# The complement masks of the second attention layer move to GpSimd, and its values are split by their upper halves

## What is computed

```python
seq = (x @ W_seq).reshape(N, H, DH)                      # N 2048, H 16, DH 32
score1 = jnp.einsum('nhd,d->hn', seq, a1)
score2 = jnp.einsum('nhd,d->hn', seq, a2)
scores = score1[:, :, None] + score2[:, None, :]
scores = jax.nn.leaky_relu(scores, negative_slope=0.2)
scores = scores + (1.0 - adj)[None, :, :] * MASK_VAL     # MASK_VAL -65500
attn = jax.nn.softmax(scores, axis=-1)
hidden = jnp.einsum('hij,jhd->ihd', attn, seq).reshape(N, D_IN)
hidden = hidden @ W_out + b_out
return jax.nn.elu(hidden)
```

## Time and profile before

| | us |
|---|---|
| median of 3 runs | 1329.88 |
| lowest, highest | 1329.02, 1330.25 |
| the profiled execution | 1327.29 |
| its span in the trace | 1325.7 |
| PE busy | 1152.6 (87%) |
| DVE busy | 974.9 (74%) |
| ACT busy | 797.1 (60%) |
| POOL busy | 169.9 (13%) |

### The profile page before, as it was taken

One profiled execution on the slowest core, in us unless ns is written; L12 is line 12 of the kernel. 1 busy time (PEld: TensorE's weight loads), 2 busy tenths in 40 slices (PEclk: granted clock), 3 DMA queues, 4 the chain that ended last, 5 costly groups with the idle time before them and its releaser, 6 DMA issues. The chain is left out here.

```text
span 1325.7 us, 24575 instructions
## 1 busy us (share of the span) xinstructions
PE 1152.6 (87%) x10450; PEld 784.7 (59%) x10450; DVE 974.9 (74%) x1340; ACT 797.1 (60%) x779; POOL 169.9 (13%) x182
## 2 busy tenths in 40 slices
PE   4797668889888888888699399999999999999797
PEld 3343323333333333334355299999999999999543
DVE  2310137999999999988189679999889988999265
ACT  1321526556665556553144588888888888888032
POOL 2777700000000000000066100000000000000011
PEclk9899789998898898899899699999999999999799
DMA  9530151221112110000476210000110000000321
GB/s 358 73 25 1 20 113 18 42 42 37 39 34 42 34 35 34 17 16 24 128 177 109 74 34 34 34 34 34 44 55 34 34 34 34 34 34 3 112 111 71
DMA packets 31625, 75.00 MB, mean 57 GB/s; under 512 B 5413, under 2 KB 10402, under 8 KB 29474
## 3 DMA queue, kind: packets, MB, share of 16 engines
q1 hardware_dynamic: 21426, 49.53, 10.7%
q0 software_dynamic: 10096, 23.97, 10.5%
HBM read 78.76 MB, written 15.61 MB: 71 GB/s over the span
## 5 line engine op out<-in xcount | busy, mean ns | idle before, releaser
L959 ACT ACTIVATE s_masks<-s_s1b,s 128x2048 fp8e4<-128x2048 f32 x208 | 396.7, 1987 | 0.0
L1104 PE MATMUL psum<-s_V,s_masks 128*128 128x198 bf16 x2560 | 352.3, 249 | 15.2 <-DVE s_masks L1001 15.2
L1105 PE MATMUL psum<-s_V,nadjT 128*128 128x99 bf16 x2560 | 347.0, 209 | 0.0
L1104 PEld LDWEIGHTS psum<-s_V,s_masks 128*128 128x128 fp8e4 x2560 | 249.9, 98 | 15.7 <-issue 15.4
L1105 PEld LDWEIGHTS psum<-s_V,nadjT 128*128 128x128 fp8e4 x2560 | 250.2, 98 | 0.0
L461 PE MATMUL psum<-h,s_WT 128*128 128x512 f32 x512 | 246.1, 606 | 0.6
L502 ACT ACTIVATE s_exp<-s_exp,s_negm 128x1536 f32<-128x1536 f32 x96 | 150.7, 1570 | 101.3 <-DVE s_negm L597 101.3
L441 PE MATMUL psum<-f_qk 64*128 64x512 f32 x576 | 159.5, 693 | 54.9 <-DVE s_negm L597 54.9
L1001 DVE TENSOR_TENSOR s_masks<-s_masks,adjT 128x512 uint32<-128x512 uint32 x256 | 169.4, 681 | 49.5 <-ACT s_masks L959 47.0
L597 DVE CUSTOM_DVE_ANT_0 s_exp<-psum,f_low 128x1536 f32<-128x1536 f32 x96 | 164.7, 1752 | 16.7 <-PE psum L441 16.2
L588 DVE SCALAR_TENSOR_TENSOR s_W<-s_exp,s_r,s_W 128x1536 f32<-128x1536 f32 x96 | 174.4, 1817 | 2.2
(11 more groups left out here) (127 smaller groups left out, 1140.5 us busy)
## 6 DMA issues: line engine op xcount, KB each, us to landing
s_s1b<-s_rows SPq DMA_DIRECT2D x16, 1024.0 KB, 4.6
s_adj<-in_adj POOLq DMA_DIRECT2D x16, 512.0 KB, 5.2
rel_planes<-s_zero POOLq DMA_DIRECT2D x3, 2304.0 KB, 23.0
f_rel<-rel_planes SPq DMA_DIRECT2D x36, 192.0 KB, 3.5
s_x<-x SPq DMA_DIRECT2D x6, 1024.0 KB, 11.0
h<-in_x SPq DMA_DIRECT2D x4, 1024.0 KB, 21.1
f_adj<-in_adj POOLq DMA_DIRECT2D x16, 256.0 KB, 5.5
s_x<-in_x SPq DMA_DIRECT2D x16, 256.0 KB, 2.6
```

Of the source, the lines that this page charges most:

```text
L959: act.activation(masks[:, j, :], s1b[b][:, :], ACT.Relu, bias=t["s2"][:, n, 0, j:j + 1], scale=BIG, saturate=False).then_inc(signs, 1)
L1104: pe.matmul(out, masks[:, j, cols], V[:, b, j, :, :], **first)
L1105: last = pe.matmul(out[:, :, DZ:CZ], nadjT[:, j, cols], V[:, b, j, :, DZ:CZ], **then)
```

## The change

In stage 3, `negated_adj` and `nadjT` go. In stage 4:
- POOL makes the far mask of every source tile as a 32-bit add of `adjT` and the mask (`far`), after `mask_ready` of that tile. A byte 0x40 + 0x40 is 0x80, which is minus zero; 0x40 + 0 is 2.0. No carry crosses a byte. The far masks are positive now, so `join` adds.
- PE does two short products for every source tile and waits for `far_ready` at each.
- `VECTOR_SIGN` is (2, 6, 10, 14): four compares on DVE, twelve on ACT.
- The split is by the upper 16 bits of each f32 (`upper`, a bf16 view with a step of two of the now doubled `tmp`): ACT copies upper halves into `V` (`pack`), DVE takes the upper half off without waiting for that copy. PE waits for `split` and `packed`.
- The places of sums, scale, join, invert, norm and take-offs among the masks move.

```diff
-VECTOR_SIGN = (3, 8, 13)
-FAR = (1, 4, 6, 9, 11, 14)
+VECTOR_SIGN = (2, 6, 10, 14)
@@ stage3, vector queue
-            def negated_adj(it):
-
-                dve.wait_ge(adj_out_a, it.at(1))
-                dve.wait_ge(adj_out_v, it.at(1))
-                dve.tensor_scalar(nadjT[:, :, it.rows()].bitcast(U32), adjT[:, :, it.rows()].bitcast(U32),
-                                  SIGNS, None, ALU.bitwise_xor).then_inc(t["lasting"], 1)
@@ stage4
-    tmp = sb("tmp", [P, NT, CZ])
+    tmp = sb("tmp", [P, 2, NT, CZ])
+    upper = tmp[:, :, :, :].bitcast(BF16).rearrange("p s j (c w) -> p s j c w", w=2)[:, :, :, :, 1]
-    fars = sb("fars", [P, len(FAR), N], F8)
+    fars = sb("fars", [P, NT, N], F8)
@@ gpsimd queue
+            def far(n, j):
+
+                pool.wait_ge(mask_ready, NT * n + j + 1)
+                pool.tensor_tensor(fars[:, j, :].bitcast(U32), adjT[:, j, :].bitcast(U32),
+                                   masks[:, j, :].bitcast(U32), ALU.add).then_inc(far_ready, 1)
+            for n in range(HB):
+                for j in range(NT):
+                    far(n, j)
@@ scalar queue
-                act.activation(V[:, b, :, p, :], tmp[:, :, :], ACT.Copy).then_inc(hi_out if p == 0 else mid_out, 1)
+                act.activation(V[:, b, :, p, :], upper[:, p, :, :], ACT.Copy).then_inc(packed, 1)
-                    if j in (5, 11) and n < HB - 1:
-                        part(n + 1, 1 - b, 0 if j == 5 else 1)
+                    if j in (9, 14) and n < HB - 1:
+                        pack(n + 1, 1 - b, 0 if j == 9 else 1)
@@ vector queue
-                    dve.wait_ge(split, m)
+                    dve.wait_ge(packed, 2 * m - 1)
+                    dve.wait_ge(rest, m)
@@ take_off
-                dve.wait_ge(hi_out if p == 0 else mid_out, m + 1)
-                out = tmp[:, :, :] if p == 0 else V[:, b, :, 2, :]
-                dve.tensor_tensor(out, tmp[:, :, :], V[:, b, :, p, :], ALU.subtract).then_inc(rest if p == 0 else split, 1)
+                dve.wait_ge(*((value, 2 * (m + 1)) if p == 0 else (rest, m + 1)))
+                if p == 0 and m > 0:
+                    dve.wait_ge(packed, 2 * m)
+                    dve.wait_ge(split, m)
+                if p == 1 and m >= 2:
+                    dve.wait_ge(psum_done[1], m - 1)
+                out = tmp[:, 1, :, :] if p == 0 else V[:, b, :, 2, :]
+                dve.tensor_tensor(out, tmp[:, p, :, :], upper[:, p, :, :], ALU.subtract).then_inc(rest if p == 0 else split, 1)
-            def far(n, j):
-
-                dve.wait_ge(mask_ready, NT * n + j + 1)
-                dve.tensor_tensor(fars[:, FAR.index(j), :].bitcast(U32), nadjT[:, j, :].bitcast(U32),
-                                  masks[:, j, :].bitcast(U32), ALU.bitwise_xor).then_inc(far_ready, 1)
@@ join
-                dve.tensor_tensor(hid[:, :, :], sums[:, :, 0, :], sums[:, :, 1, :], ALU.subtract).then_inc(joined, 1)
+                dve.tensor_tensor(hid[:, :, :], sums[:, :, 0, :], sums[:, :, 1, :], ALU.add).then_inc(joined, 1)
@@ head: j of sum_parts 0, scale, join, invert, norm: 2, 7, 8, 9, 11 -> 3, 13, 14, 15, 15; take-offs 6, 12 -> 9, 11
@@ tensor queue
-                if j in FAR:
-                    pe.wait_ge(far_ready, len(FAR) * n + FAR.index(j) + 1)
+                pe.wait_ge(far_ready, NT * n + j + 1)
-                    if j in FAR:
-                        pe.matmul(out[:, :, 0:DZ], masks[:, j, cols], V[:, b, j, :, 0:DZ], **first)
-                        last = pe.matmul(out[:, :, DZ:CZ], fars[:, FAR.index(j), cols], V[:, b, j, :, DZ:CZ], **then)
-                    else:
-                        pe.matmul(out, masks[:, j, cols], V[:, b, j, :, :], **first)
-                        last = pe.matmul(out[:, :, DZ:CZ], nadjT[:, j, cols], V[:, b, j, :, DZ:CZ], **then)
+                    pe.matmul(out[:, :, 0:DZ], masks[:, j, cols], V[:, b, j, :, 0:DZ], **first)
+                    last = pe.matmul(out[:, :, DZ:CZ], fars[:, j, cols], V[:, b, j, :, DZ:CZ], **then)
@@ head
                 pe.wait_ge(split, n + 1)
+                pe.wait_ge(packed, 2 * (n + 1))
```

More of the change, by code:

```diff
@@ L57 @@
 NEAR = 2.0
-SIGNS = 0x80808080
 ADJ_RING = 6
@@ L643, in stage3 @@
     sem = lambda name: c.enter_context(nc.semaphore(name))
-    seq, adjT, nadjT = t["seq"], t["adjT"], t["nadjT"]
+    seq, adjT = t["seq"], t["adjT"]
     xs = sb("s3_x", [P, NT, D])
@@ L779, in _ @@
                 score(At(0, n - 2))
-                negated_adj(At(0, n - 2))
             score(At(0, NT - 2))
-            negated_adj(At(0, NT - 2))
             turned_adj(At(0, NT - 1))
             score(At(0, NT - 1))
-            negated_adj(At(0, NT - 1))
             steps_done = [0]
@@ L925, in stage4 @@
         sem("signs"), sem("vector_signs"), sem("mask"), sem("far"), sem("mask_used"))
-    value, hi_out, rest, mid_out, split = sem("value"), sem("hi"), sem("rest"), sem("mid"), sem("split")
+    value, rest, split, packed = sem("value"), sem("rest"), sem("split"), sem("packed")
     psum_done, bank_free = ([sem(f"{n}{i}") for i in range(2)] for n in ("psum_done", "bank_free"))
@@ L939, in _, with pack @@
                 load(n + 2, n % 2)
+        @block.gpsimd
+        def _(pool):
+            def far(n, j):
[5 more added lines that the diff above has]
+                    far(n, j)
         @block.scalar
         def _(act):
-            def part(m, b, p):
+            def pack(m, b, p):
                 act.wait_ge(*((value, 2 * (m + 1)) if p == 0 else (rest, m + 1)))
@@ L960, in head @@
                                        saturate=False).then_inc(signs, 1)
-                    if j in (5, 11) and n < HB - 1:
-                        part(n + 1, 1 - b, 0 if j == 5 else 1)
-            part(0, 0, 0)
-            part(0, 0, 1)
+                    if j in (9, 14) and n < HB - 1:
+                        pack(n + 1, 1 - b, 0 if j == 9 else 1)
+            pack(0, 0, 0)
+            pack(0, 0, 1)
             for n in range(HB):
@@ L975, in values @@
                 if m > 0:
-                    dve.wait_ge(split, m)
-                dve.tensor_tensor(tmp[:, :, :].rearrange("p j (k z) -> p j k z", k=2)[:, :, :, 0:DH],
-                                  seq[:, :, None, m * DH:(m + 1) * DH].to_broadcast([P, NT, 2, DH]),
+                    dve.wait_ge(packed, 2 * m - 1)
+                    dve.wait_ge(rest, m)
+                out = tmp[:, 0, :, :].rearrange("p j (k z) -> p j k z", k=2)
+                dve.tensor_tensor(out[:, :, :, 0:DH], seq[:, :, None, m * DH:(m + 1) * DH].to_broadcast([P, NT, 2, DH]),
                                   t["e"][:, :, :, m:m + 1].rearrange("p k j o -> p j k o").to_broadcast([P, NT, 2, DH]),
                                   ALU.mult).then_inc(value, 1)
-                dve.tensor_copy(tmp[:, :, :].rearrange("p j (k z) -> p j k z", k=2)[:, :, :, DH:DZ],
-                                t["e"][:, :, :, m:m + 1].rearrange("p k j o -> p j k o")).then_inc(value, 1)
+                dve.tensor_copy(out[:, :, :, DH:DZ], t["e"][:, :, :, m:m + 1].rearrange("p k j o -> p j k o")).then_inc(value, 1)
             def take_off(m, b, p):
-                dve.wait_ge(hi_out if p == 0 else mid_out, m + 1)
-                out = tmp[:, :, :] if p == 0 else V[:, b, :, 2, :]
-                dve.tensor_tensor(out, tmp[:, :, :], V[:, b, :, p, :], ALU.subtract).then_inc(rest if p == 0 else split, 1)
+                dve.wait_ge(*((value, 2 * (m + 1)) if p == 0 else (rest, m + 1)))
[6 more added lines that the diff above has]
+                dve.tensor_tensor(out, tmp[:, p, :, :], upper[:, p, :, :], ALU.subtract).then_inc(rest if p == 0 else split, 1)
             def vector_sign(n, b, j):
@@ L1047, in head @@
                     mask(n, j)
-                    if j - 1 in FAR:
-                        far(n, j - 1)
                     if n > 0:
-                        if j == 2:
+                        if j == 3:
                             sum_parts(n - 1, 0)
@@ L1054, in head @@
                             sum_parts(n - 1, 1)
-                        if j == 7:
+                        if j == 13:
                             scale(n - 1)
-                        if j == 8:
+                        if j == 14:
                             join(n - 1)
-                        if j == 9:
+                        if j == 15:
                             invert(n - 1)
-                        if j == 11:
                             norm(n - 1)
@@ L1065, in head @@
                             values(n + 1)
-                        if j == 6:
+                        if j == 9:
                             take_off(n + 1, 1 - b, 0)
-                        if j == 12:
+                        if j == 11:
                             take_off(n + 1, 1 - b, 1)
@@ L1287, in build @@
                     sb = lambda name, shape, dt=F32: attention.enter_context(nc.sbuf_tensor(name, shape, dt))
```

(2 more changed lines are left out.)

## The result

The changed kernel takes 1457.59 us (median of 4 runs, 1456.5 to 1458.78); the kernel before, run beside it, 1330.07. The ratio is 1.0958 (95% interval 1.0939 to 1.0977): 127.5 us slower. Forecast were 1469 us and 139 us slower.

What follows compares the result with a forecast made beforehand. PE bounds stage 4 at 30.0 us a head; DVE and POOL excluding each other would make it 39.4. The last reduction then comes 139.6 us later, less 0.3 in stage 3: 1466.6, 1469 as median; range 1370 to 1620.

Steps and rivals of the forecast that it cites:

- PE's sum: Stage 4: all 32 steps of a head become short, 24.0 us, 5.8 us less; alone worth 93 us.
- The inference on the port: Stage 4: whatever fetches two SBUF words a cycle, two-input DVE instructions too, can't run beside a POOL product or add.
- The word rates drawn from rows 7 and 8: DVE's two-input instructions, L765 and compares fetch two words in about 1.05 to 1.1 ns; reductions fetch one.
- T: Full stage 4 head: 20.2 us of DVE port work, 20.0 of POOL, handovers -1.9, reductions +1.1; 39.4 us.
- the port's work: DVE work of a stage 4 head that excludes POOL's: 24.1 less reductions, reciprocal and small copy, 20.2 us.
- The integer add: POOL's add in stage 4 costs what stage 3's product does: 1.25 us each, 20.0 us a head.
- Rivals 2 and 4: Stage 4 add dearer, from 1.6 us, 1559 us total (chance 0.08); or as cheap as DVE's, 0.60, no change (0.03).
- ACT's copies with a step: Stage 4 copies reading every second bf16 keep their price, 0.97 us, within 0.5 either way.
- Start of stage 4: Take-off 0 no longer waits for ACT's copy; first mask at about 752.4, some 1.1 us sooner.
- Stage 3: Dropping sixteen L765 from DVE gains nothing, as PE bounds the loop; only the last one saves 0.3 us.
- Rival 3: PE in stage 4 cools to its lower clock throughout, 48.0 us a head, 1607 us in total; chance 0.05.
- PE's waits: In stage 4 PE waits in every source tile for its far masks, as a sign of the forecast.

## Why the prediction was right

*What bounds, PE's sum.* Right. The short steps alone, shown without the adds, gave 85 us where the sum had 93 for PE alone and ACT's 24.9 us a head as the next bound; the head came to 24.5.

*The inference on the port.* Right, and now shown rather than argued: a two-input instruction is held by a reading POOL instruction (masks of 1318 ns), it is not by a writing one (691 ns), and reductions aren't by either. The word rates drawn from rows 7 and 8 pointed the right way. They were incomplete on one point: I spoke of "two SBUF words a cycle" fetched and of nothing else, while the compares and the copy are held by a POOL that reads nothing. For those, POOL's writing is enough.

*The size.* T was put at 39.4 us and is 38.7. The terms: DVE without POOL 24.1 against 24.5 (without adds; ACT is busy throughout there, so that run alone is no test to 0.4 us). Most of this is the reductions: I took 1.8 us for each, and from start to start one takes 1.95 (917.13 to 919.08). POOL's add was 1.25 less 0.12 of handover, 1.13, and is 1.07. 20.2 + 16 x 1.07 + 1.1 = 38.4 us; the 0.3 that are missing are twice the 0.15 of the reductions. So T holds two errors of opposite sign, 16 x 0.06 = 1.0 us on the adds and 0.3 on the reductions, and comes out 0.7 too long; a part of its closeness is luck. The small copy, which I left out of the port's work, is held too; at 0.09 us it changes nothing in the sum. Fourteen full heads at 0.7 us less make 9.8 of the 10.2 us between 139.6 forecast and 129.4 measured for the last reduction.

*The integer add.* It costs what the product did: 1257 ns at its shortest, against 1253 for the product. Rivals 2 and 4 are out.

*ACT's copies with a step.* 1084 ns for 1077: no price, inside the bounds given.

*Start of stage 4.* The first mask came at 753.0, not 752.4, so 0.5 us sooner than the 753.52 of before and not 1.1: ACT's first compare had to wait 0.45 us for the DMA of the s1 row, which had been hidden behind the old, longer chain of splits. A step that I had not followed to its next releaser; 0.6 us.

*Stage 3.* Right that it gains nothing:

```profile
680.00:690.00 10.00, 10.00 (x58) 5.73 (x57) 6.37 (x9) 4.42 (x6) 6.65 (x7) 1.00 0.66 110
```

PE 10.00 of 10.00 as in rows 10, DVE 6.37 instead of 9.70. Wrong in the last 0.3 us: the step behind the last L765 starts at 742.73 as against 742.69, because what ended last there was POOL's reduction over the partitions, which starts at 742.30 and 742.27. The 0.3 us were hidden; I had taken the end of DVE's row for the path.

*Rival 3, PE cools.* PE's clock is 0.93 in the stretch with PE busy for 70%, and 0.90 with eight adds; without gaps it is 1.00. It falls a little, and a short matmul takes 216 ns instead of 209, but PE has 30% of spare time.

*PE's waits.* They were forecast for every source tile. In the stretch from 850 to 1300 us PE waits for a far mask 112 times in 186 tiles, 131 us in all: the right queue, and not every tile.

*Not run.* A DVE instruction with one SBUF input and one word a cycle beside the adds, other than the reductions, wasn't tried; nor what decides which of the two engines gets the port when both wait.

## What to carry to other kernels

Before moving elementwise work from DVE to POOL, add the port times of both, not the engine times: every DVE instruction with two SBUF inputs and those like the compares and the copy, plus every POOL instruction that reads. Here work of 0.60 us on DVE cost DVE 1.07 us once POOL did it (0.89 in the mean of sixteen), with both engines' own sums well below the bound. POOL is free where DVE works from PSUM: put its instruction so that it comes due there (two of them, with seven far masks kept on DVE, gave the quickest of the kernels run), and let it write only where it can.

## What was not expected of the hardware

- A copy of 32 words a partition, 0.19 us alone, took 1.25 us in the median of the changed kernel: a small instruction waits as long as a large one.
- The handover gives time back: a mask and an add in turn take 1.67 us, while alone their pitches are 0.60 and 1.25, 1.85 together. I read this as start-up that whichever is held has behind it when the port comes free; no run tests it.
- A POOL memset of 1472 words takes 1.32 us in the quickest rows and holds only the compares and the small copy: at 96% busy POOL cost the kernel 16 us in all, where at 77% with adds it cost 210. The held copy of 32 words delays nothing there: at 1018.36 it takes 0.93 us, and the next mask starts at 1018.45.
